# A fused cross-attention and mixture-of-experts layer: low parts of the up weights made ahead, one shared batch moved behind the experts, tables moved

## The chip, the cores and the metric

The kernel runs on one core of a Trainium2 chip. The metric is the device time of one execution in microseconds (us). The core has TensorE (PE, matmuls; PEld is its weight load), VectorE (DVE), ScalarE (ACT), GpSimd (POOL) and SyncE (SP, which here only issues DMAs). Each runs its own instructions in order and waits for the others by semaphores. DMAs are issued from SP's, ACT's and POOL's queues.

## The reference, cut to what matters

```python
x = x + cross_attention(layernorm(x), ctx, ctx)     # x: 4 x 512 x 256, 16 heads, causal: the first 512 context rows count
xf = layernorm(x).reshape(2048, 256)
top, idx = top_k(xf @ gate_w.T, 2)                  # 8 experts, 2 for each row
comb = zeros(2048, 8).at[rows, idx].add(softmax(top))
for e in range(8):                                  # w_up: 8 x 768 x 256 (gate and up), w_down: 8 x 256 x 384
    y = silu(xf @ wg[e].T) * (xf @ wu[e].T) @ w_down[e].T
    out = out + comb[:, e:e + 1] * y
shared = silu(xf @ sg_gate.T) * (xf @ sg_up.T) @ sg_down.T
return x + (shared + out).reshape(4, 512, 256)
```

All inputs and outputs are fp32. There are four batches of 512 rows.

## The kernel before

**Attention** (to about 265 us) takes the heads in NG = 4 groups of four, batch after batch. A loop (`Fori`) runs batches 0 to 2, the last batch is written out by itself. On each engine a function `batch` (PE L767, ACT L1093, DVE L1331, SP L407) holds its part. PE's work of a group is a `slot` (L710): row-maximum scores of the next group (L624, L626) that DVE reduces (L1306) and splits in `max_parts` (L1308), transposed scores of this group (L644) that ACT exponentiates (L1074, `exps`), probabilities times values of the group before (L654) and, near the end of the slot, the maxima's matmuls (L634). The score banks of PE are a ring of three: block j waits until ACT has freed block j - 3. In slots g = 1 and g = 3 of the loop there are also projections (L675) and ACT's and POOL's splitting of their results (`part1`, `part2`, `part3`, ACT L995), whose pieces SP copies into place (`stack`, L390). SP loads one third of the down weights at the end of each loop batch (L432). In the last batch ACT copies the down weights in six pieces to fp32r (`down_hi`, L1059, called out of `exps` after blocks 3 and 7), and DVE subtracts to get the low parts (`down_lo`, L1326).

**Parts.** An fp32 matmul is two instructions in the profile. The experts' matmuls are instead made of fp32r parts: a high part (a copy to fp32r) and a low part (the rest); three matmuls, high x high, high x low and low x high, stand for one.

**The front of the experts** (about 265 to 327 us). `ln2_transposes` and `logits` give the router's input; DVE makes ranks, tiles and slots in a long chain (L1399 to L1504), `in_tile` (L1472), `at_tile` (L1476, L1477) and 32 columns `at_slot` (`hot_slots`, L1480, L1483); PE turns them into lists by 32 matmuls (L898), DVE reduces them to `token_of` (L1504). POOL then gathers rows by indirect DMA (L580). The normalised rows are stored to DRAM first (`xn_d`: SP L445 for batches 0 to 2, ACT L1134 for batch 3), and with them 16 bytes a row of router results (`who`, SP L452). SP loads the up weights (6 MB, `wup`, L450) as soon as attention has let go of their place; ACT copies them to high parts (`hi_parts`, eight pieces), DVE subtracts low parts (`lo_part`, L1486). Meanwhile PE computes the shared expert of batches 0, 1 and 2: `shared_up` (L844; gate and up, three blocks m of four fp32 matmuls on 512 columns, L851), ACT's silu (L1146), DVE's product (`shared_h`, L1405), `shared_down` (L855, 12 fp32 matmuls on 256 columns, L861), DVE's addition (`shared_y`, L1410).

**The expert slots** (327 to 476 us). 39 tiles of 128 gathered rows; in slot t PE transposes the rows of tile t + 1 (L910), transposes hidden of t - 2 (L933), does `down` of t - 3 (nine matmuls of 256 columns, L942 to L944) and `up` of t (12 matmuls of 384 columns, L923 to L925). ACT makes the high parts and the silu, DVE the low parts, the product and the weighted result; POOL adds the results into one of two sums in DRAM (L588).

**The end** (from 476 us). PE does the shared expert of batch 3, SP loads the two sums (L458), DVE adds them (`add_sum`, L1593), adds the shared result (L1606), and ACT stores the output (L1211).

The order that PE's front has, in full (its waits and calls from L890 to L955):

```python
shared_up(0, 2); pe.wait_ge(rank_read, 2); shared_down(0); shared_up(1)
pe.wait_ge(hot_built, 1)          # then the 32 matmuls of the lists
shared_down(1); shared_up(2, 0, 2)
pe.wait_ge(hot_read, 1)
rows_t(0, 0, 0, 1, True); shared_up(2, 2, 3); rows_t(1, 1, 1, 1); shared_down(2)
pe.wait_ge(up_lo, SPLITS)         # then up(0, 0, first[0])
```

Of the kernel before, what the change touches and what calls it, by code (L numbers as in the profile page):

```python
# [28 lines left out]
P = 128  # L29
F32 = mybir.dt.float32  # L30
# [14 lines left out]
def build(nc, x, ctxT, wqT, bq, wkT, bk, wvT, bv, woT, bo, gwT, wupT, wdnT, sgT, suT, sdT, out):  # L45
# [34 lines left out]
    with ExitStack() as ctx:  # L80
# [9 lines left out]
        xn_d = nc.dram_tensor("normed_rows", (N + P, D + WHO), F32, kind="Internal").ap()  # L90
        acc = [nc.dram_tensor(f"sum_rows{i}", (N + P, D), F32, kind="Internal").ap() for i in range(2)]
# [10 lines left out]
        wdn_lo = sb("w_down_lo", [P, M, E * D], F32R)  # L102
        wsg = sb("w_sg", [P, C, HALF])
# [28 lines left out]
        with nc.sbuf_tensor("e_hT_hi", [P, 2, M, P], F32R) as e_hT_hi, \  # L132
                nc.sbuf_tensor("e_hT_lo", [P, 2, M, P], F32R) as e_hT_lo:
            pass
        moe = sb("moe", [P, MOE])
        e_xT_hi = sb("e_xT_hi", [P, 2, C, P], F32R)
# [5 lines left out]
        with nc.sbuf_tensor("ahead_of_router", [P, 24 * KB], F32) as ahead:  # L142
            with nc.sbuf_tensor("router", [P, 24 * KB], F32) as router:
                pass
        ROUTER = 24 * KB
        wup_hi = sb("wup_hi", [P, C, E * 2 * HALF], F32R)
        with nc.sbuf_tensor("wup", [P, C, E * 2 * HALF], F32) as wup:
            pass
        wup_lo = sb("wup_lo", [P, C, E * 2 * HALF], F32R)
        wdn_hi = sb("w_down_hi", [P, M, E * D], F32R)  # L150
# [86 lines left out]
        in_tile = part(NJ * NT // 2).bitcast(BF16).rearrange("p (j t) -> p j t", j=NJ)  # L237
# [3 lines left out]
        tcmp = hot[:, NT * E:2 * NT * E].rearrange("p (t e) -> p t e", e=E)  # L241
        at_tile = part(NJ * NCOL * NT // 2).bitcast(BF16).rearrange("p (j c t) -> p j c t", j=NJ, c=NCOL)
# [3 lines left out]
        ld_k, ld_q, ld_ctx, ld_v, ld_o, ld_cv, ld_moe, ld_up = (sem(n) for n in  # L246
            ("ld_k", "ld_q", "ld_ctx", "ld_v", "ld_o", "ld_cv", "ld_moe", "ld_up"))
        consts, pads, fills, pad_rows = sem("consts"), sem("pads"), sem("fills"), sem("pad_rows")
        xn_stored, acc_zeroed = sem("xn_stored"), sem("acc_zeroed")
# [31 lines left out]
        up_hi, up_lo, wts_ready, e_xhi = (sem(n) for n in ("up_hi", "up_lo", "wts_ready", "e_xhi"))  # L281
# [65 lines left out]
        EARLY = 4  # L347
# [1297 lines left out]
```

## Time and profile before

| | |
|---|---|
| median of 3 runs | 501.17 us (499.0 to 502.9) |
| the profiled execution | 502.17 us, its span 500.3 us |
| TensorE busy | 458.4 us, 92% of the span |
| VectorE, ScalarE, GpSimd busy | 308.2, 210.1, 193.1 us |
| mean granted TensorE clock | 0.982 of full speed |

The profile shows one execution; its times are microseconds from the start of the span. A line number such as L851 is a line of the kernel before. "Busy" counts the time in which an engine has an instruction at work; matmuls are pipelined, so the starts of two neighbours tell more of a matmul's cost than its own duration. The granted clock is a share of TensorE's full speed, 2.4 GHz. In a timeline row the bracket at the end is the idle time before the instruction and what ended it.

### The profile page before, as it was taken

The page shows a single profiled execution, that of the slowest core. Times are in us where ns is not written, and L with a number is a line of the kernel's source. Part 1 is how long each engine was busy: PE and PEld are TensorE (multiplying, and loading weights), DVE is VectorE, ACT ScalarE, POOL GpSimd, SP SyncE. Part 2 cuts the span into 40 slices and gives each one's busy share as a digit, 9 for nine tenths or more (in the row PEclk, how much of TensorE's full clock was granted, in tenths as well). Part 3 has the DMA queues.
Part 4 walks back from the last instruction along what each step waited for, and adds up shares of the span by engine and source line. Part 5 has one row for each costly group of instructions (what it writes and reads, how often), then busy time and mean ns, then how long its engine had stood idle before and what let it go on. Part 6 is the DMA issues. An engine that isn't in the chain of part 4 may idle for free.

```text
span 500.3 us, 10299 instructions
## 1 busy us (share of the span) xinstructions
PE 458.4 (92%) x3154; PEld 318.9 (64%) x3155; DVE 308.2 (62%) x651; ACT 210.1 (42%) x420; POOL 193.1 (39%) x204
## 2 busy tenths in 40 slices
PE   7868999999999999988699799999999999999993
PEld 6644344654447443554256366599999999999852
DVE  4984757477563757656674796855554554555436
ACT  2254666517572566517862352523322322322210
POOL 4123545114541336201512002126666766665420
PEclk9998999999999999999979899999999999999998
DMA  8593322422124121400298900014344344444279
GB/s 263 102 229 107 108 72 65 149 65 73 64 78 145 33 95 47 138 28 2 77 371 292 367 2 21 21 33 65 64 74 74 63 71 70 70 65 74 33 197 338
DMA packets 45574, 53.84 MB, mean 108 GB/s; under 512 B 7760, under 2 KB 41872, under 8 KB 44912
## 3 DMA queue, kind: packets, MB, share of 16 engines
q1 hardware_dynamic: 34320, 39.77, 24.8%
q0 software_dynamic: 7488, 10.31, 12.8%
q10 hardware_dynamic: 3744, 3.47, 2.7%
q8 instruction: 13, 0.21, 0.2%
q14 instruction: 9, 0.07, 0.1%
HBM read 27.09 MB, written 13.67 MB: 81 GB/s over the span
## 4 chain that ended last, share of the span: by engine, by line
PE 68%; DVE 10%; ACT 9%; DMA 6%; issue 5%; SPq 1%; DVEq 0%; ACTq 0%; POOLq 0%
PE set_a L624 7%; PE set_b L654 7%; PE set_a L924 6%; PE set_a L925 5%; PE set_a L923 5%; ACT attention L1074 5%; PE set_a L851 5%; PE set_a L675 4%; PE set_b L644 4%; DVE attention L1306 3%; PE set_b L861 3%; PE set_b L942 3%; PE set_a L832 3%; PE set_b L943 3%; PE set_b L944 3%
## 5 line engine op out<-in xcount | busy, mean ns | idle before, releaser
L1306 DVE TENSOR_REDUCE attention<-set_a 128x2 f32<-128x1024 f32 (+2 forms) x96 | 95.9, 1042 | 28.0 <-PE set_a L626 26.1
L1074 ACT ACTIVATE attention<-set_b 128x512 f32<-128x512 f32 (+1 forms) x176 | 88.4, 570 | 58.5 <-PE set_b L644 45.8
L528 POOL TENSOR_SCALAR_AFFINE_SELECT attention<-attention 128x512 f32<-128x512 f32 x64 | 40.8, 650 | 110.4 <-ACT attention L1074 110.4
L588 POOL DMA_INDIRECT sum_rows<-moe,token_of x39 | 61.8, 1585 | 43.9 <-issue 28.9
L644 PE MATMUL set_b<-attention 99*128 99x512 bf16 (+3 forms) x256 | 60.4, 310 | 13.6 <-ACT attention L1074 10.2
L624 PE MATMUL set_a<-attention 96*128 96x512 bf16 (+3 forms) x256 | 61.5, 306 | 5.6 <-DVE attention L1306 5.4
L580 POOL DMA_INDIRECT e_x<-normed_rows,token_of x39 | 39.4, 1010 | 63.7 <-DVE token_of L1504 37.3
L1173 ACT ACTIVATE moe<-set_a 128x384 f32<-128x384 f32 x39 | 19.1, 490 | 104.9 <-PE set_a L925 104.9
L1529 DVE TENSOR_TENSOR moe<-set_a,moe 128x384 f32<-128x384 f32 x39 | 21.8, 558 | 62.7 <-ACT moe L1173 62.7
L624 PEld LDWEIGHTS set_a<-attention 96*128 96x128 bf16 x256 | 25.3, 99 | 45.3 <-DVE attention L1306 18.0
L923 PE MATMUL set_a<-wup_hi,e_xT_hi 128*128 x156 | 53.1, 340 | 0.0
L924 PE MATMUL set_a<-wup_lo,e_xT_hi 128*128 x156 | 52.9, 339 | 0.0
L925 PE MATMUL set_a<-wup_hi,e_xT_lo 128*128 x156 | 52.8, 338 | 0.0
L626 PE MATMUL set_a<-maskb,identb 128*128 128x128 bf16 x256 | 49.6, 222 | 0.0
L654 PE MATMUL set_b<-attention 128*32 128x128 f32 (+3 forms) x512 | 46.2, 463 | 0.4 <-ACT attention L995 0.3
L644 PEld LDWEIGHTS set_b<-attention 99*128 99x128 bf16 x256 | 19.6, 99 | 37.2 <-ACT attention L1074 24.8
L942 PE MATMUL set_b<-w_down_hi,e_hT_hi 128*128 x117 | 36.4, 311 | 1.3 <-DVE moe L1541 0.8
L995 ACT ACTIVATE attention<-set_b 12x512 bf16<-12x512 f32 (+4 forms) x48 | 25.7, 596 | 22.6 <-PE set_b L820 10.2
L509 POOL TENSOR_TENSOR attention<-attention 128x512 f32<-128x512 f32 x14 | 15.9, 1154 | 47.5 <-ACT attention L995 27.8
L944 PE MATMUL set_b<-w_down_hi,e_hT_lo 128*128 x117 | 32.9, 281 | 0.0
L943 PE MATMUL set_b<-w_down_lo,e_hT_hi 128*128 x117 | 32.9, 281 | 0.0
L995 ACT ACTIVATE attention<-attention 128x512 bf16<-128x512 f32 x32 | 19.4, 644 | 30.9 <-DVE attention L1254 26.2
(167 smaller groups left out, 843.5 us busy)
## 6 DMA issues: line engine op xcount, KB each, us to landing
attention<-attention SPq DMA_DIRECT2D x182, 64.0 KB, 2.6
wup<-in_wupT SPq DMA_DIRECT2D x2, 3072.0 KB, 14.6
sum_rows<-attention SPq DMA_DIRECT2D x2, 2048.0 KB, 13.6
wup<-sum_rows SPq DMA_DIRECT2D x8, 512.0 KB, 7.0
attention<-in_ctxT SPq DMA_DIRECT2D x7, 512.0 KB, 6.2
w_down<-in_wdnT SPq DMA_DIRECT2D x3, 1024.0 KB, 5.0
x_res<-in_x SPq DMA_DIRECT2D x4, 512.0 KB, 7.1
out<-x_res ACTq DMA_DIRECT2D x8, 256.0 KB, 4.0
```

The lines of the kernel that those rows point to most:

```text
L588: g.indirect_dma_start(acc[i], bass.IndirectOffsetOnAxis(token_of[:, t:t + 1], 0), e_y[:, t % 2, :], None, compute_op=ALU.add).then_inc(ad ...
L624: mm(dst, qstack[0:ROWS, g // 2, h, k * P:w], kstack[0:ROWS, g // 2, h, 0:w], start=True, stop=False)
L626: last = mm(dst[:, k * P:w], identb[:], maskb[:], start=False, stop=True)
L644: last = mm(bank(par)[:, i * w:(i + 1) * w], kstack[0:ROWS + 3, g // 2, h, k * P:(k + 1) * P], qstack[0:ROWS + 3, g // 2, h, k * P:S], sta ...
L654: last = mm(pv_bank[32 * h:32 * h + 32, k * P:S], vaug[:, k, HG * g + h, :], pT[k][:, h, :], start=k == 0, stop=k == QT - 1, tile_position ...
L923: mm(dst, e_xT_hi[:, a, c, :], wup_hi[:, c, cols], start=c == 0, stop=False)
L924: mm(dst, e_xT_hi[:, a, c, :], wup_lo[:, c, cols], start=False, stop=False)
L925: last = mm(dst, e_xT_lo[:, a, c, :], wup_hi[:, c, cols], start=False, stop=c == C - 1)
L942: mm(dst, e_hT_hi[:, a, m, :], wdn_hi[:, m, cols], start=m == 0, stop=False)
L943: mm(dst, e_hT_hi[:, a, m, :], wdn_lo[:, m, cols], start=False, stop=False)
L1074: nc.scalar.activation(pT[k][:, h:h + heads, :], bank(par)[:, 0:heads * (S - k * P)], ACT.Exp).then_inc(b_free, 1)
L1306: v.tensor_reduce(dst, src, AX.X, ALU.max, negate=True).then_inc(a_free, 1)
```

## The change

**Up weights' low parts.** In each of the loop's three batches SP loads a third of the up weights (2 MB) into a place of attention's that was free (`ahead`, which shares its memory with `wdn_hi`). In slots g = 2 and g = 3 ACT copies two pieces each to fp32r (`ahead_part`, 128 x 1024, after blocks 2 and 6 of `exps`), and DVE subtracts two pieces each behind `max_parts` (`ahead_low`). SP then stores the low parts (2 MB) to a tensor in DRAM (`up_lo_d`). At the front SP loads them (2 x 3 MB) behind the two loads of `wup`; `lo_part` is gone from DVE, and ACT makes the high parts in one go between the silus of batches 0 and 1.

**Third shared batch.** Batch 2's shared expert moves behind the expert slots, ahead of batch 3's. Gate and up of these two are made of fp32r parts (`shared_up_parts`: 36 matmuls of 512 columns a batch, where 12 fp32 ones were). Their high parts (rows and weights) are four copies on ACT in slots 4 to 7, their low parts four subtractions on DVE in slots 5 to 8; these slots are taken out of the loops.

**Tables.** `at_slot`, `tio`, `tcmp`, `in_tile` and `at_tile` move from memory of their own onto the normalised rows, `at_tile` onto those of batch 3. POOL's `tio` waits for the stores of batches 0 to 2, and DVE waits for that of batch 3 (`xn_last`) ahead of `at_tile`. The `who` store moves from SP's queue to ACT's, behind that of batch 3.

```diff
...
+        sg_end = wup[:, 0, T * D:T * D + M * S].rearrange("p (m n) -> p m n", m=M)
+        x_lo = moe_r[:, T * D:T * D + C * N].rearrange("p (c n) -> p c n", c=C)
+        x_hi = [at.rearrange("p (c n) -> p c n", c=C) for at in
+                (moe_r[:, T * D - C * S:T * D], moe_r[:, T * D + N:T * D + N + C * S])]
+        w_hi = moe_r[:, T * D + C * N:T * D + C * N + 2 * C * HALF].rearrange("p (a c n) -> p a c n", a=2, c=C)
...
+        parts_of(moe, (B - 1) * QT * D)
         hot = part(NJ * P // 2)
         at_slot = hot.bitcast(BF16).rearrange("p (j i) -> p j i", j=NJ)
         tio = hot[:, 0:NT * E].rearrange("p (t e) -> p t e", e=E)
         tcmp = hot[:, NT * E:2 * NT * E].rearrange("p (t e) -> p t e", e=E)
+        in_tile = part(NJ * NT // 2).bitcast(BF16).rearrange("p (j t) -> p j t", j=NJ)
+        size[0] = T * D
         at_tile = part(NJ * NCOL * NT // 2).bitcast(BF16).rearrange("p (j c t) -> p j c t", j=NJ, c=NCOL)
...
+        def ahead_piece(w, k):
+            c, half = divmod(k, AHEAD // C)
+            return w[:, c, half * W_AHEAD // 2:(half + 1) * W_AHEAD // 2]
+
+        def ahead_high(k):
+            return wdn_hi[:, C, k % 2 * W_AHEAD // 2:(k % 2 + 1) * W_AHEAD // 2]
...
+                    sp.dma_start(ahead[:, 0:C, :], wupT.rearrange("(c p) n -> p c n", p=P)[:, :, bass.ds(b * W_AHEAD, W_AHEAD)]
+                                 ).then_inc(ahead_in, DMA)
...
+                    sp.wait_ge(ahead_lo, AHEAD * (b + 1))
+                    sp.dma_start(up_lo_d[:, :, bass.ds(b * W_AHEAD, W_AHEAD)], wdn_hi[:, 0:C, :].bitcast(F32)
+                                 ).then_inc(ahead_out, DMA)
                     sp.wait_ge(b_full, n_b + 3 * B_SLOT)
                     stack(3, 2 * b + 3)
+                    sp.wait_ge(ahead_out, DMA * (b + 1))
                     sp.dma_start(wdn[:, bass.ds(b, 1), :], wdnT[bass.ds(b * P, P)].rearrange("p (o n) -> p o n", o=1)
...
-                sp.dma_start(wup[:, c, :], wupT[c * P:(c + 1) * P]).then_inc(ld_up, DMA)
-            sp.wait_ge(who_ready, TOP_K)
-            sp.dma_start(xn_d[0:N, D:D + WHO].rearrange("(t p) i -> p t i", p=P), who).then_inc(who_stored, DMA)
+                sp.dma_start(wup[:, c, :], wupT[c * P:(c + 1) * P]).then_inc(ld_up[c], DMA)
+            for c in range(C):
+                sp.dma_start(wup_lo[:, c, :].bitcast(F32), up_lo_d[:, c, :]).then_inc(ld_lo, DMA)
...
+            pool.wait_ge(xn_stored, DMA * (B - 1))
+            pool.wait_ge(b_full, B_LN2[2] + C)
+            count(tio, [[1, NT], [0, E]], 0, 0)
 
 
             pool.wait_ge(pad_rows, DMA)
             pool.wait_ge(acc_zeroed, 2 * DMA)
-            pool.wait_ge(xn_stored, DMA * B)
+            pool.wait_ge(xn_last, DMA)
...
+            def shared_up_parts(b):
                 for m in range(M):
+                    n = b * M + m
+                    pe.wait_ge(s_h, n - 1)
+                    for i, (w_lo, dst) in enumerate(zip((wsg_lo, wsu_lo), gu[n % 2])):
+                        for c in range(C):
+                            high, low = w_hi[:, i, c, m * P:(m + 1) * P], w_lo[:, c, m * P:(m + 1) * P]
+                            rows_hi, rows_lo = x_hi[b - 2][:, c, :], x_lo[:, c, b * S:(b + 1) * S]
+                            mm(dst, high, rows_hi, start=c == 0, stop=False)
+                            mm(dst, high, rows_lo, start=False, stop=False)
+                            last = mm(dst, low, rows_hi, start=False, stop=c == C - 1)
+                    last.then_inc(s_up, 1)
...
-            shared_up(1)
+            shared_up(1, 0, 2)
...
             last.then_inc(hot_full, 1)
-            shared_down(1)
-            shared_up(2, 0, 2)
+            shared_up(1, 2)
...
+            shared_down(1, 0, 1)
             rows_t(0, 0, 0, 1, True)
-            shared_up(2, 2, 3)
+            shared_down(1, 1, 2)
             rows_t(1, 1, 1, 1)
-            shared_down(2)
+            shared_down(1, 2)
             pe.wait_ge(experts_known, 1)
             first = [expert(t) for t in range(3)]
-            pe.wait_ge(up_lo, SPLITS)
-            pe.wait_ge(s_h, (B - 1) * M)
+            pe.wait_ge(up_hi, SPLITS)
+            pe.wait_ge(ld_lo, DMA * C)
+            pe.wait_ge(s_h, (B - 2) * M)
             up(0, 0, first[0])
...
-            shared_up(3)
+            pe.wait_ge(end_lo, AHEAD)
+            shared_up_parts(2)
             pe.wait_ge(e_yr, NT + 1)
+            shared_down(2)
+            shared_up_parts(3)
             shared_down(3)
...
+            def ahead_part(b, k):
+                if k == 0:
+                    act.wait_ge(ahead_in, DMA * (b + 1))
+                if k > 1:
+                    act.wait_ge(ahead_lo, AHEAD * b + k - 1)
+                copy(ahead_high(k), ahead_piece(ahead, k)).then_inc(ahead_hi, 1)
...
+                                  b, {2: 2 * g - 4, 6: 2 * g - 3} if g > 1 and not final else {})
...
+                                xn2[:, (B - 1) * QT:T, :]).then_inc(xn_last, DMA)
...
+            shared_silu(0, 0)
+            shared_silu(0, 1)
+            act.wait_ge(who_ready, TOP_K)
+            nc.scalar.dma_start(xn_d[0:N, D:D + WHO].rearrange("(t p) i -> p t i", p=P), who).then_inc(who_stored, DMA)
+            shared_silu(0, 2)
+            act.wait_ge(ld_up[0], DMA)
+            hi_parts(range(0, SPLITS // 2))
+            act.wait_ge(ld_up[1], DMA)
+            hi_parts(range(SPLITS // 2, SPLITS - 2))
+            shared_silu(1, 0)
+            hi_parts(range(SPLITS - 2, SPLITS - 1))
+            shared_silu(1, 1)
+            hi_parts(range(SPLITS - 1, SPLITS))
+            shared_silu(1, 2)
...
+            high_of = ((x_hi[0], xn2T[:, :, 2 * S:3 * S]), (x_hi[1], xn2T[:, :, 3 * S:4 * S]),
+                       (w_hi[:, 0], wsg[:]), (w_hi[:, 1], wsu[:]))
+            for t in range(3, PEEL):
+                slot(t, t % 2)
+                if t - 4 in range(AHEAD):
+                    copy(*high_of[t - 4]).then_inc(end_hi, 1)
...
+            def ahead_low(b, k):
+                dve.wait_ge(ahead_hi, AHEAD * b + k + 1)
+                v.tensor_tensor(ahead_piece(wdn_hi, k), ahead_piece(ahead, k), ahead_high(k),
+                                ALU.subtract).then_inc(ahead_lo, 1)
...
+                    if g in (2, 3) and not final:
+                        for k in (2 * g - 4, 2 * g - 3):
+                            ahead_low(b, k)
...
             shared_h(0, 2)
+            dve.wait_ge(xn_last, DMA)
             v.tensor_tensor(at_tile[:, :, 0, :], in_tile, per_row(row_of), ALU.mult)
             v.tensor_tensor(at_tile[:, :, 1, :], in_tile, per_row(own_lo), ALU.mult)
...
-            shared_y(1)
-
-            lo_part(2)
-            shared_h(2, 0)
-            lo_part(3)
-            lo_part(EARLY)
-            shared_h(2, 1)
+            shared_h(1, 2)
...
+            def end_low(i):
+                dve.wait_ge(end_hi, i + 1)
+                dst, src, high = ((x_lo[:, :, 2 * S:3 * S], xn2T[:, :, 2 * S:3 * S], x_hi[0]),
+                                  (x_lo[:, :, 3 * S:4 * S], xn2T[:, :, 3 * S:4 * S], x_hi[1]),
+                                  (wsg_lo[:], wsg[:], w_hi[:, 0]), (wsu_lo[:], wsu[:], w_hi[:, 1]))[i]
+                v.tensor_tensor(dst, src, high, ALU.subtract).then_inc(end_lo, 1)
...
+                shared_h(2, m)
+            for b in range(B - 2):
+                add_sum(1, slice(b * QT, (b + 1) * QT), (y_in[1][b], DMA))
+            shared_y(2)
+            shared_h(3, 0)
+            dve.wait_ge(s_yfree, B)
+            add_sum(1, slice(2 * QT, 3 * QT), (y_in[1][2], DMA))
+            shared_h(3, 1)
             add_sum(1, slice(T - QT, T), (y_in[1][B - 1], DMA))
+            shared_h(3, 2)
             for c in range(2 * B):
...
```

## Rows read from the trace of the kernel before

**Rows 1.** The page: busy us of each engine, share, instructions.

```profile
PE 458.4 (92%) x3154; PEld 318.9 (64%) x3155; DVE 308.2 (62%) x651; ACT 210.1 (42%) x420; POOL 193.1 (39%) x204
```

**Rows 2.** Windows: length, busy us of each engine, granted clock, DMA share, GB/s.

```profile
284.00:286.00 2.00, 2.00 (x4) 0.86 (x3) 1.81 (x6) 0.00 (x0) 0.00 (x0) 0.53 0.68 226
...
360.00:380.00 20.00, 20.00 (x140) 19.68 (x139) 10.19 (x30) 5.94 (x16) 13.36 (x11) 1.00 0.45 74
```

**Rows 3.** Chain that ended last, in time: start, us, engine, tile, line.

```profile
283.03 5.40 PE set_a L851 x8
...
293.61 10.30 PE set_a L851 x24
...
321.88 5.18 PE set_b L861 x24
...
327.06 0.18 PE set_a L923
...
335.16 0.12 PE set_b L943
```

**Rows 4.** Timeline of ACT in attention: start, us, engine, line, shapes, idle before.

```profile
115.34 1.19 ACT L995 ACTIVATE attention<-attention 128x512 bf16<-128x512 f32 x2
...
123.17 2.62 ACT L1074 ACTIVATE attention<-set_b 128x512 f32<-128x512 f32 x6 [0.64 <-PE set_b L644]
...
238.53 1.06 ACT L995 ACTIVATE w_down_hi<-w_down 128x1024 fp32r<-128x1024 f32 x1
```

**Rows 5.** Timeline of the end, PE and DVE.

```profile
476.01 1.88 PE L851 MATMUL set_a<-moe,w_sg 128*128 128x512 f32 x4
...
491.65 1.29 DVE L1593 TENSOR_TENSOR x_res<-x_res,wup 128x512 f32<-128x512 f32 x2 [0.21 <-DMA wup<-sum_rows]
...
495.84 1.28 DVE L1606 TENSOR_TENSOR x_res<-set_b,x_res 128x512 f32<-128x512 f32 x2
```

**Rows 6.** Timeline of DVE in attention.

```profile
130.75 1.41 DVE L1254 TENSOR_SCALAR attention<-set_a,attention 128x512 f32<-128x512 f32 x2 [5.04 <-PE set_a L675]
...
240.01 5.06 DVE L1328 TENSOR_TENSOR w_down_lo<-w_down,w_down_hi 128x1024 fp32r<-128x1024 f32 x4
```

**Rows 7.** Timeline of PE: maxima matmuls around two slots g = 2.

```profile
115.79 0.39 PE L634 MATMUL set_b<-identb,attention 128*12 128x128 bf16 x4
...
126.07 0.39 PE L634 MATMUL set_b<-identb,attention 128*12 128x128 bf16 x4
...
230.27 0.39 PE L634 MATMUL set_b<-identb,attention 128*12 128x128 bf16 x4
...
241.40 0.39 PE L634 MATMUL set_b<-identb,attention 128*12 128x128 bf16 x4
```

**Rows 8.** Timeline of the front, ACT's queue, DVE and POOL.

```profile
272.77 0.41 ACTq L1134 DMA_DIRECT2D normed_rows<-moe  x1
...
290.70 1.45 DVE L1476 TENSOR_TENSOR router<-router 128x1248 bf16<-128x1248 bf16 x1
...
299.06 1.39 DVE L1483 TENSOR_SCALAR router<-router 128x128 bf16<-128x128 bf16 x8
...
307.12 0.24 DVE L1504 TENSOR_SCALAR token_of<-router 128x39 int32<-128x39 f32 x1
...
308.30 1.15 POOL L580 DMA_INDIRECT e_x<-normed_rows,token_of  x1 [37.27 <-DVE token_of L1504]
```

**Rows 9.** Tile wup: issue (ns, first and last start) and landing (us).

```profile
L450 SPq DMA_DIRECT2D wup<-in_wupT x2: 345/390/434, 268.4 to 268.8; - x2
...
DMA to landing us min/median/max: 10.3/14.6/18.8
```

**Rows 10.** DMA queues, 281 to 284 (packets, MB, share); issue, 268 to 273.

```profile
q1 hardware_dynamic: 48, 1.18, 107.6%
q10 hardware_dynamic: 48, 0.05, 5.4%
...
normed_rows<-moe ACTq DMA_DIRECT2D x1, 512.0 KB, 16.6
```

More of the change, by code:

```diff
@@ L134, in build @@
             pass
+        with nc.sbuf_tensor("moe_parts", [P, MOE], F32R) as moe_r:
+            pass
         moe = sb("moe", [P, MOE])
+        ROUTER = 2068
+        with nc.sbuf_tensor("router", [P, ROUTER], F32) as router:
+            pass
         e_xT_hi = sb("e_xT_hi", [P, 2, C, P], F32R)
@@ L139, in build @@
         e_w = sb("e_w", [P, 2, TOP_K])
[L142 to L146, printed above, removed]
         with nc.sbuf_tensor("wup", [P, C, E * 2 * HALF], F32) as wup:
             pass
+        wup_hi = sb("wup_hi", [P, C, E * 2 * HALF], F32R)
         wup_lo = sb("wup_lo", [P, C, E * 2 * HALF], F32R)
+        with nc.sbuf_tensor("up_ahead", [P, M, E * D], F32) as ahead:
+            pass
         wdn_hi = sb("w_down_hi", [P, M, E * D], F32R)
@@ L1201, in _ @@
             hidden_t(NT - 1, (NT - 1) % 2)
-            for m in range(M):
-                shared_silu(3, m)
+            for b in range(B - 2, B):
+                for m in range(M):
+                    shared_silu(b, m)
             o_t = out.rearrange("b (k p) d -> p (b k) d", p=P)
@@ L1546, in freed @@
                 return added[i], DMA * SUMS[i][t - 1]
[L1548 removed]
             rows_lo(0, 0)
[L1550 to L1551 removed]
             rows_lo(1, 1)
[L1553 removed]
             weights(0, 0, True)
             weights(1, 1, True)
[L1556 removed]
+            shared_y(1)
             hidden(0, 0)
@@ L1571, in slot @@
                 hidden(t, a)
-            for t in range(3, 5):
-                slot(t, t % 2, (t + 1) % NX, None)
-            LOOPS = (NT - 7) // NX
+            def end_low(i):
[4 more added lines that the diff above has]
+                v.tensor_tensor(dst, src, high, ALU.subtract).then_inc(end_lo, 1)
+            PEEL = 9
+            for t in range(3, PEEL):
+                slot(t, t % 2, (t + 1) % NX, freed(t - 3) if t > 4 else None)
+                if t - 5 in range(AHEAD):
+                    end_low(t - 5)
+            LOOPS = (NT - 1 - PEEL) // NX
             with dve.Fori(0, LOOPS) as i:
                 for j in range(NX):
-                    slot(NX * i + 5 + j, (5 + j) % 2, (6 + j) % NX, (added[j % 2], DMA * (2 * i + j // 2 + 1)))
-            for t in range(5 + NX * LOOPS, NT - 1):
+                    slot(NX * i + PEEL + j, (PEEL + j) % 2, (PEEL + 1 + j) % NX,
+                         (added[j % 2], DMA * (2 * i + 2 + j // 2 + 1)))
+            for t in range(PEEL + NX * LOOPS, NT - 1):
                 slot(t, t % 2, (t + 1) % NX, freed(t - 3))
```

83 lines of the change are left out of this document (35 added, 48 removed).

## Prediction, made before the change was run

> **What bounds the kernel now.** I read four views in this order. The page's engine line says that TensorE is busy for 92% of the span [rows 1]. The windows by stage say where that is hard: in the expert slots PE is busy for 20.00 of 20 us, with VectorE at 10.2 and ScalarE at 5.9 [rows 2]. The chain of waits then shows the stretch between attention and experts: from 283.03 to the first expert matmul at 327.06 it is almost all shared-expert matmuls [rows 3], so there too PE is the limit, and the router's lists are ready before PE has time for them. In attention PE is close to full, but its banks are freed by ScalarE's exponentials, which run six in a row with nothing between them [rows 4]; a copy put among them is paid by PE. At the tail the last thing is VectorE's two additions at 495.84, some four microseconds after PE has finished (476.01 + 10.3 + 5.2 = 491.5), because the sums' loads and additions are longer than PE's work there [rows 3, 5]. So four stretches count: attention, the front (283 to 327), the expert slots, the end. The trace's run took 502.17 us for a span of 500.3 and the median of the runs is 501.17; I sum against 502.17 and take off 1.0 for the median.
>
> **Attention: low parts made ahead.** In each of the three loop batches, slots g = 2 and g = 3 get two ScalarE copies and two VectorE subtractions of 128x1024. Both have exact twins in the last batch: one down_hi copy takes 1.06 us [rows 4], and four down_lo subtractions take 5.06 us, some 1.23 each [rows 6]. What a pair of such copies does to a slot can be read from the same slot (g = 2) with and without them, from one set of maxima to the next: 126.07 - 115.79 = 10.28 us in the loop, 241.40 - 230.27 = 11.13 us in the last batch [rows 7]. That is 0.85 us for the pair, but an underestimate: the loop's slot before it already holds part2's two copies (1.19 us [rows 4]) just before its maxima, where the last batch has its second copy, so that copy is partly cancelled. The ceiling is that nothing hides: 2 x 1.06 = 2.12 a slot. Over six slots this is 5.1 to 12.7 us. I take 1.5 a slot, 9.0 us, in the middle: the first copy sits in the run of six, and the second delays the exponential on which the maxima and the last two score blocks wait; in g = 3 it comes on top of part2. It could be nothing only if ScalarE had idle time inside the run, and it has none. The subtractions I cost at nothing: VectorE idles 5.04 us between the end of the maxima's parts and its next operation in g = 2 [rows 6], against 2 x 1.23; if that cover fails, 3 x 2 x 1.23 = 7 us. SP gets a 2 MB load, a wait for the fourth subtraction, a 2 MB store and a wait for it, per batch. Behind the first wait stand the stack DMAs of group 3, which are not needed before slot g = 2 of the next batch, two slots and the batch's own projections later; behind the second the w_down load and the next context load, which are needed later still. Nothing.
>
> **The front: what leaves it.** Batch 2's gate and up (10.30 us for 24 instructions) and down (5.18) leave PE ahead of the experts, 15.5 us [rows 3]; eight subtractions leave VectorE. If the rest kept up, PE would finish gate and up of batch 1's first two blocks at 300.5, build the lists at once, get its first gathered rows at 306 to 307 and start the experts near 312, that is 15 us sooner.
>
> **The front: what ends last in its place.** The tables for the lists move onto the rows of batch 3, so VectorE now waits for their store (xn_last) ahead of the operation that ran at 290.70 [rows 8]. That store is issued on ScalarE's queue at 272.77 [rows 8], while SP's queue is loading the 6 MB of wup, issued at 268.4 and 268.8 [rows 9]. The store took 16.6 us to land [rows 10], at 289.4; the second half of wup took 18.8 [rows 9], to 287.6. So the 0.5 MB landed only when the 6 MB were through. The packet counts say why: in the 3 us from 281, SP's queue moved 48 packets (1.18 MB, 24 KB each) and ScalarE's 48 (0.05 MB, 1 KB each) [rows 10]. They alternate one for one, 16 a microsecond each, and the store has 512 packets. Now 6 MB of low parts follow wup in SP's queue in the same 24 KB rows: 256 packets more, 16 us at that rate, to about 303.5. At 16 a microsecond from 274 on the store alone needs until 306. So it lands with the end of the low parts, near 304.5, and VectorE stands there for 14 us. Behind the wait are the two at_tile products, the 32 hot columns, shared_y(0) and shared_h(1, 0); PE waits for hot_built from 300.5 on, ScalarE for PE, and GpSimd for the lists.
>
> From the operation at 290.70 to the last hot column at 300.45 VectorE worked without a gap, 9.75 us [rows 8]: hot_built comes at 304.5 + 9.75 = 314.3. PE has stood for 14 us by then. After a much shorter stand, just ahead of 283.03, the granted clock was 0.53 from 284 to 286 [rows 2], the lower of the two levels (1.2 GHz), and eight instructions took 5.40 where 3.43 (a third of 10.30) is usual [rows 3]: 2 us lost. So: lists 2.4 after hot_built, gathers 0.95 after token_of is done (308.30 against 307.12 + 0.24 [rows 8]), first rows about 3 us later, at 320.5; PE meanwhile runs batch 1's third gate and up at the lower clock, 316.1 to 321.5, then down and the two transposes, 5.8 us: first expert matmul at 327.3. Before it was 327.06. I put the front at 0, between -3 (no clock loss, store 1 us sooner) and +4. The who store moves behind xn_last on the same queue and is through by 308, ahead of the lists.
>
> **A rule against that.** The rows show one 1 KB packet to one 24 KB packet [rows 10]. The Trainium skill, page "DMA: Bandwidth & Descriptors", section "Queues, rings and completion order", says that a DMA engine takes turns between queues a packet at a time, and that such a packet holds typically some 9 to 17 descriptors. By that rule the store's 32 rows per engine would need 2 to 4 turns of the other queue, land by about 279 and hold nobody up. It landed at 289.4, which speaks against it here; what it would give is the first rival.
>
> **The expert slots.** Four copies and four subtractions go into peeled slots. A slot is some 3.8 us (476.01 less 327.06, over 39) with ScalarE at 30% and VectorE at 51% [rows 2], so each (about 1.06 and 1.23) fits beside PE. I take 0.3 in all; the ceiling is 4 us. The loops' other parts are the same.
>
> **The end.** Batch 2 joins batch 3 behind the experts. A matmul of 384 columns in fp32r takes 0.18 us and one of 256 columns 0.12 [rows 3], so I estimate 0.24 for 512; 36 of them are 8.6 us a batch, in place of 10.30 (7.7 if 0.18 and 0.12 hold a fixed part that doesn't grow). PE then has 8.6 + 5.2 + 8.6 = 22.4 us to the end of the last gate and up, and silu and product take 1.4 more. Behind that product VectorE has eight additions of 0.65 (1.29 for two [rows 5]), 5.2, as long as the last down on PE: the final additions start 29.0 us after the last expert matmul. Before, they started at 495.84 - 476.01 = 19.8 us after it [rows 5]. That is +9.2; with 0.3 off, since the last output store no longer shares the queue with seven others, +8.9 (7.3 to 10). Before, PE's extra work would have been covered for 4 us by the sums' loads; I have counted that cover as used up.
>
> **Sum.** 9.0 + 0 + 0.3 + 8.9 = 18.2: 502.17 + 18.2 = 520.4, less 1.0 for the median: 519.
>
> **Rivals.** (A) The store isn't late: its rows go several to a turn while the low parts load, VectorE goes on at 290.7, the front gains 15 and the sum is 519 - 15 = 504, no change that can be told. What decides is whether xn_last lands before 291. For it: by 289.4 it had landed in the run before, so little has to improve; against it, the 48 to 48 and the 16.6 us. (B) The store is late, but the attention copies are hidden, at 1.5 us in all: 511.5, still slower; against it, the 0.85 a slot of the last batch. (C) One cover for both: ScalarE's copies fall into time that PE owes to others and the store lands early: 504 - 8 = 496, faster. It needs A and B together. (D) The front is worse, with PE at the lower clock into the first slots: 523.
>
> **Chances.** The forecast (with D) 0.60, A 0.17, B 0.10, C 0.13. About 1% (5 us) is what a measurement of this kernel can tell from no change. So slower by over 1% is forecast, D and B, 0.70; within 1% A, 0.17; faster C, 0.13. The range takes in all but C and the low edge of A: 503 to 525; the likeliest case alone has 513 to 525.
>
> **What would show it.** VectorE idle for some 14 us, ended by the store to the normalised rows, ahead of the product at at_tile; PE idle from gate and up of batch 1 to the lists' matmuls, then a granted clock near 0.5; first expert matmul (relative to the end of attention) where it was; slots g = 2 and 3 of the loop 1 to 2 us longer each; 29 us between the last expert matmul and the final additions. A first expert matmul 10 us or more earlier would make the forecast wrong, and so would slots g = 2 of 10.28 us as before.

## The result, and the profile after

The changed kernel takes 524.59 us (median of 4 runs, 523.13 to 525.69), beside 501.22 us for the kernel before on the same chip. The ratio is 1.0467, with a 95% interval of 1.0419 to 1.0516: slower by 4.7%, where 519 was forecast. Its profiled execution took 524.41 us for a span of 522.5, so the span grew by 22.2.

Four marks cut both spans into the stages that the prediction used: the start of attention's last addition into `x_res`, the first and the last expert matmul, and the end of the span. The stages were read in this way in every kernel that follows:

| kernel | median us | attention, to its last addition | front, to the first expert matmul | expert slots | end | span |
|---|---|---|---|---|---|---|
| before | 501.2 | 267.1 | 59.6 | 149.2 | 24.4 | 500.3 |
| after | 524.6 | 281.1 | 58.2 | 150.8 | 32.4 | 522.5 |
| difference | | +14.0 | -1.4 | +1.6 | +8.0 | +22.2 |
| predicted | | +9.0 | 0 | +0.3 | +8.9 | +18.2 |

The engine line of the page, and the window of 24 us in the expert slots (columns as in [rows 2]):

```profile
PE 458.9 (88%) x3178; PEld 324.8 (62%) x3179; DVE 314.7 (60%) x659; ACT 224.4 (43%) x436; POOL 195.9 (37%) x204
```

```profile
356.00:380.00 24.00, 23.20 (x155) 21.83 (x154) 16.81 (x42) 9.97 (x24) 15.48 (x12) 1.00 0.41 67
```

PE has as many busy microseconds as in [rows 1] (458.4), in a longer span: what was added is waiting, not work. In the expert slots that prepare the end's parts it is busy for 23.20 of 24 us, where it had no gap before [rows 2].

**Attention.** Maxima matmuls mark the slots, as in [rows 7]. First the timeline of PE in the changed kernel, around a slot g = 2, a slot g = 3 and the slot behind it:

```profile
123.00 0.39 PE L666 MATMUL set_b<-identb,attention 128*12 128x128 bf16 x4
...
132.46 0.72 PE L676 MATMUL set_b<-attention 99*128 99x384 bf16 x2 [1.09 <-ACT attention L1134]
...
134.22 0.39 PE L666 MATMUL set_b<-identb,attention 128*12 128x128 bf16 x4
...
148.88 0.39 PE L666 MATMUL set_b<-identb,attention 128*12 128x128 bf16 x4
...
151.10 0.40 PE L676 MATMUL set_b<-attention 99*128 99x128 bf16 x4 [1.13 <-ACT attention L1134]
...
160.10 0.39 PE L666 MATMUL set_b<-identb,attention 128*12 128x128 bf16 x4
```

Attention's last addition, on DVE's timeline (267.12 before):

```profile
281.09 1.23 DVE L1449 TENSOR_TENSOR x_res<-set_a,x_res 128x1024 f32<-128x1024 f32 x1 [4.64 <-PE set_a L864]
```

Then what ScalarE does in the slot g = 2:

```profile
130.37 0.60 ACT L1134 ACTIVATE attention<-set_b 128x512 f32<-128x512 f32 x1 [0.64 <-PE set_b L676]
130.87 1.05 ACT L1047 ACTIVATE w_down_hi<-up_ahead 128x1024 fp32r<-128x1024 f32 x1
131.81 1.73 ACT L1134 ACTIVATE attention<-set_b 128x512 f32<-128x512 f32 x4
133.40 1.09 ACT L1047 ACTIVATE w_down_hi<-up_ahead 128x1024 fp32r<-128x1024 f32 x1
```

The same marks, and the same block, in the kernel before ([rows 7] has the mark at 126.07):

```profile
124.31 0.72 PE L644 MATMUL set_b<-attention 99*128 99x384 bf16 x2 [0.15 <-ACT attention L1074]
...
139.35 0.39 PE L634 MATMUL set_b<-identb,attention 128*12 128x128 bf16 x4
...
149.63 0.39 PE L634 MATMUL set_b<-identb,attention 128*12 128x128 bf16 x4
```

The slot from 123.00 takes 11.22 us (10.28 before). The two copies stand among the exponentials, and PE's score block at 132.46 waits 1.09 us for one of these; in the kernel before, the same block waits 0.15. The difference, 0.94, is the whole growth of the slot. The slot g = 3 takes 14.66 instead of 13.28, and the one behind it, which begins with the second copy's delay (1.13 against 0.57 at its first blocks, after 0.32 more), 11.22 instead of 10.28. Together 3.26 a loop batch, 9.8 in three. That leaves 4.2 of the 14.0. Batch 0 has the rest: its slot g = 2 takes 16.61 us, 5.4 more than the same slot of batch 1. PE's timeline there, with the first matmul after a gap, and then the windows before and after that:

```profile
56.61 0.39 PE L666 MATMUL set_b<-identb,attention 128*12 128x128 bf16 x4
...
64.72 0.60 PE L676 MATMUL set_b<-attention 99*128 99x512 bf16 x1 [2.89 <-DMA attention<-attention]
...
73.22 0.59 PE L666 MATMUL set_b<-identb,attention 128*12 128x128 bf16 x4
```

```profile
56.60:65.00 8.40, 4.94 (x40) 1.88 (x40) 3.41 (x3) 3.21 (x7) 3.98 (x5) 0.97 0.97 208
65.00:75.00 10.00, 9.80 (x57) 5.25 (x56) 6.32 (x9) 7.22 (x13) 2.02 (x2) 0.51 0.19 57
```

PE waits 2.89 us for a DMA in attention, and then runs ten microseconds at 0.51, the lower of its two levels. The matmul after the gap is the first transposed score of the slot, which by the kernel's code waits for the row of the slot's maxima (`max_in`): a DMA of 12 KB that ScalarE issued at 58.75.

```profile
58.75 0.77 ACTq L1090 DMA_DIRECT2D attention<-attention  x1
```

Up to that gap the DMA engines are full (0.97). The issues of 47 to 60 us (KB each, median us to landing) say with what: SP's 2 MB load, issued at 49.50, has gone ahead of SP's stack DMAs, which landed in 2.8 us in this stretch of the kernel before and land in 5.8 now.

```profile
up_ahead<-in_wupT SPq DMA_DIRECT2D x1, 2048.0 KB, 10.0
attention<-attention SPq DMA_DIRECT2D x14, 64.0 KB, 5.8
```

The two queues' packets (number, MB, share) in the 6 us from the issue of the small DMA show it among these:

```profile
q1 hardware_dynamic: 1140, 0.95, 98.2%
q10 hardware_dynamic: 15, 0.01, 1.3%
```

Its 15 packets go in two parts, ten before 62 and five after 63; in the kernel before, the 15 of the same DMA went within 0.3 us. Why the second part came so much later no run shows.

(The first slots of batch 0 happened to be 1.5 shorter than before and the last batch 0.2 longer: 9.8 + 5.4 - 1.5 + 0.2 = 14.0, to a tenth.)

**The front.** The timeline of the stretch that [rows 3, 8] show for the kernel before, and then the issues of the two stores:

```profile
286.62 0.41 ACTq L1197 DMA_DIRECT2D normed_rows<-moe  x1
...
317.68 1.46 DVE L1558 TENSOR_TENSOR moe<-moe,router 128x1248 bf16<-128x1248 bf16 x1 [13.05 <-DMA normed_rows<-moe]
...
327.50 2.26 PE L946 MATMUL set_b<-moe 128*128 128x78 bf16 x32 [13.32 <-DVE moe L1565]
...
339.33 0.43 PE L970 MATMUL set_a<-wup_hi,e_xT_hi 128*128 x1
```

```profile
normed_rows<-moe ACTq DMA_DIRECT2D x1, 512.0 KB, 31.0
normed_rows<-router ACTq DMA_DIRECT2D x1, 32.0 KB, 23.7
```

The store of batch 3's rows, issued at 286.62, lands 31.0 us later; VectorE stands 13.05 us for it, and PE 13.32 us for VectorE's hot columns. The queues' packets (number, MB, share) in the three microseconds from 294 and from 309 show why: SP's queue, with rows of 24 KB, and ScalarE's, with rows of 1 KB, move 48 and 48. In the single microsecond from 294 they move 16 and 16, one row of each on each of the 16 engines.

```profile
q1 hardware_dynamic: 48, 1.18, 92.5%
q10 hardware_dynamic: 48, 0.05, 5.3%
...
q1 hardware_dynamic: 48, 1.18, 91.4%
q10 hardware_dynamic: 48, 0.05, 4.6%
```

From 315 on, when the loads are through, what is left in ScalarE's queue moves alone: 1744 packets in 3 us but 0.05 MB, the last rows of the store and the 16-byte rows of the `who` store behind it. The store lands at 317.6. So 13 us of standing replaces the 15 us of shared-expert work that left [rows 3], and the first expert matmul comes 58.2 us after attention instead of 59.6.

**The end.** PE's timeline behind the last expert matmul, and VectorE's last additions (before: [rows 5]):

```profile
490.21 0.39 PE L895 MATMUL set_a<-moe_parts 128*128 128x512 f32 x1
490.44 0.40 PE L896 MATMUL set_a<-moe_parts 128*128 128x512 f32 x1
490.67 0.40 PE L897 MATMUL set_a<-moe_parts,w_sg_lo 128*128 128x512 f32 x1
...
518.43 1.28 DVE L1689 TENSOR_TENSOR x_res<-set_b,x_res 128x512 f32<-128x512 f32 x2
```

One fp32r product of 512 columns follows the other in 0.23 us; the last additions start 28.2 us after the first of them, where it was 19.8.

### The profile page after: what moved, and what is told of

It reads as the page before. It is cut to its first block, busy times and chain, and to the rows that moved or that the text cites. A ratio compares the mean times of both kernels' runs of the same rounds, so it can differ in the third digit from the quotient of the medians.

```text
span 522.5 us, 10358 instructions
## 1 busy us (share of the span) xinstructions
PE 458.9 (88%) x3178; PEld 324.8 (62%) x3179; DVE 314.7 (60%) x659; ACT 224.4 (43%) x436; POOL 195.9 (37%) x204
## 4 chain that ended last, share of the span: by engine, by line
PE 62%; DVE 11%; ACT 10%; DMA 9%; issue 6%; SPq 1%; ACTq 0%; DVEq 0%
PE set_a L656 6%; DMA normed_rows<-moe 6%; ACT attention L1134 5%; PE set_a L971 5%; PE set_a L970 5%; PE set_a L972 5%; PE set_b L686 5%; PE set_a L707 4%; PE set_b L676 3%; PE set_b L989 3%; DVE attention L1378 3%; PE set_a L864 3%; PE set_b L990 3%; PE set_b L991 3%; PE set_b L980 2%
## 5 line engine op out<-in xcount | busy, mean ns | idle before, releaser
L1134 ACT ACTIVATE attention<-set_b 128x512 f32<-128x512 f32 (+1 forms) x176 | 89.5, 568 | 59.5 <-PE set_b L676 46.0
L559 POOL TENSOR_SCALAR_AFFINE_SELECT attention<-attention 128x512 f32<-128x512 f32 x64 | 44.4, 706 | 119.5 <-ACT attention L1134 119.5
L676 PE MATMUL set_b<-attention 99*128 99x512 bf16 (+3 forms) x256 | 61.7, 317 | 24.4 <-ACT attention L1134 18.3
## 6 DMA issues: line engine op xcount, KB each, us to landing
wup<-sum_rows SPq DMA_DIRECT2D x8, 512.0 KB, 6.9
attention<-in_ctxT SPq DMA_DIRECT2D x7, 512.0 KB, 8.8
```

Source lines behind the costliest of these rows:

```text
L676: last = mm(bank(par)[:, i * w:(i + 1) * w], kstack[0:ROWS + 3, g // 2, h, k * P:(k + 1) * P], qstack[0:ROWS + 3, g // 2, h, k * P:S], sta ...
L1134: nc.scalar.activation(pT[k][:, h:h + heads, :], bank(par)[:, 0:heads * (S - k * P)], ACT.Exp).then_inc(b_free, 1)
```

## The experiments

Theory after the result: three separate costs, each with its own place, make the kernel slower: the load of low parts at the front (13 us, behind which the rows' store alternates), the copies in the slots (9.8), and SP's first 2 MB load (5.4). The end costs 8, which the front's 15 would more than pay. The rivals were that the front is bound by something else behind the store, that a slot's growth comes from the subtractions or the DMAs, and that the end's new form gains nothing. The ratios are to the kernel before, measured beside the experiments: 501.98 us for the first four, 502.31 for the other three. Each stage is read from one profiled execution.

**The loads of low parts wait for the rows' store.**

```diff
             for c in range(C):
                 sp.dma_start(wup[:, c, :], wupT[c * P:(c + 1) * P]).then_inc(ld_up[c], DMA)
+            sp.wait_ge(xn_last, DMA)
             for c in range(C):
```

> The kernel after, with one wait added on SP: the loads of the low parts are issued only when batch 3's store (xn_last) has landed. My theory: that store lands late (31 us after its issue) because it shares the DMA engines with 12 MB of 24 KB rows one packet for one packet; without the second 6 MB it lands as in the kernel before, some 17 us after its issue, VectorE's 13 us wait ahead of at_tile is gone, and the experts start some 13 us sooner. The low parts then land some 16 us after the store, before PE wants them. Time: 524.6 - 13 = 511 to 512. Rival (the lists are late for another reason, such as the who store behind it or the gathers): less than 3 us gained.

512.04 us, ratio to the kernel before 1.019 (1.014 to 1.0239). The store landed 15.8 us after its issue instead of 31.0, and the front shrank from 58.2 to 44.3. So the store was what bound the front, and with it early nothing else held the experts back within these 14 us. Up to 300 us `wup` itself was still loading, and there the queues alternated as before, 49 to 48 packets in 3 us; in the 4 us from 300, with `wup` nearly through, ScalarE's queue moved 0.42 MB (2455 packets, most of them the 16-byte rows of `who`).

**The same loads in rows of 3 KB.**

```diff
-                sp.dma_start(wup[:, c, :], wupT[c * P:(c + 1) * P]).then_inc(ld_up[c], DMA)
+                for j in range(8):
+                    at = slice(j * CUT, (j + 1) * CUT)
+                    sp.dma_start(wup[:, c, at], wupT[c * P:(c + 1) * P, at]).then_inc(ld_up[c], DMA)
...
```

(The loads of `wup_lo` are cut in the same way; CUT is 768 columns.)

> The kernel after, with the loads of wup and of its low parts each cut into 8 DMAs of 768 columns (rows of 3 KB in place of 24 KB), same queue, same bytes, same order, no wait added. If the queues share packet for packet (my theory), the store of 512 rows of 1 KB needs 32 turns an engine at some 4 KB a turn, near 24 GB/s an engine: 5 to 6 us, so it lands 6 to 9 us after its issue with 12 MB still being loaded; VectorE does not wait, time 511 to 512. Rival (the queues share by bytes, or the store is held until what was issued before it is through): it still lands 17 to 31 us after its issue, and the time stays within 3 us of 524.6 or goes to 512 only through a shorter load.

511.83 us, ratio 1.019 (1.0152 to 1.0228), the front 43.7 us: as good as waiting, though nothing waits. The rows' store landed in 10.5 us, somewhat later than expected, but VectorE did not wait for it. The queues' packets in the 3 us from 294, with SP's rows now 3 KB long:

```profile
q1 hardware_dynamic: 327, 0.89, 74.0%
q10 hardware_dynamic: 322, 0.33, 30.9%
```

Again one row to one row, but ScalarE's queue now moves 0.33 MB in the time in which it moved 0.05. Here it is the length of the other queue's rows that sets how long the store of short rows takes beside it.

**Batch 0's load ahead of attention.**

```diff
+            def load_ahead(b):
+                sp.dma_start(ahead[:, 0:C, :], ...)
+
+            load_ahead(0)
...
-                    sp.dma_start(ahead[:, 0:C, :], ...)
...
-            with sp.Fori(0, B - 1) as b:
+            with sp.Fori(0, B - 2) as b:
                 batch(b, False)
+                load_ahead(b + 1)
+            batch(B - 2, False)
```

> The kernel after, with batch 0's load of up weights (2 MB) issued at the start of the program, behind the load of the values' bias, in place of at the start of batch 0; the other two stay where they were. In the trace after, slot g = 2 of batch 0 is 16.6 us from maxima to maxima where batches 1 and 2 have 11.2, with PE waiting 2.9 us on the row of maxima's DMA and a granted clock of 0.5 behind it. My theory: the 2 MB hold up the stack copies, and these hold up that small DMA on the other queue; with the load gone from there this slot is 11.2 too. Time: 524.6 - 5.4 = 519. Rival (the slot is long because ScalarE waits for the load itself, or the first pass of a loop is slow anyway): no change, or slower.

521.59 us, ratio 1.0365 (1.0321 to 1.0409). That is 3.0 us less than the changed kernel, where 5.4 was expected. Batch 0's slot g = 2 took 11.23 us, as in the other batches, and PE did not wait for the small DMA. With the load in its old place it waited 2.3 to 3.3 us in four traces of six (the changed kernel's and those of the low loads that wait, the 3 KB rows and no copies); the other two are taken up at the run without subtractions. So the load is what held that slot up. But attention ended only 1.9 us earlier: the slot behind g = 3 took 12.80 and 12.82 us instead of 11.22 in two batches. The window of one of them, below the same slot of the changed kernel:

```profile
148.88:160.10 11.22, 9.40 (x85) 4.35 (x84) 8.26 (x12) 7.96 (x17) 5.42 (x7) 1.00 0.55 219
```

```profile
145.35:158.17 12.82, 11.00 (x85) 4.72 (x84) 8.27 (x12) 7.96 (x17) 5.43 (x7) 0.87 0.58 215
```

PE is busy for 1.6 us more with as many matmuls at a clock of 0.87: the lower level, for a few microseconds. It follows the two waits for ScalarE at the slot's start (0.32 and 1.13 us); the same two waits, as long, are in the changed kernel, where the clock stayed at 1.00. In the six traces that keep the copies in the slots, 9 of the 18 slots behind a g = 3 in the loop took 12.8 us, one or two in each trace but the changed kernel's own; in the three without (before, no copies, all three places), none of nine did. So in an execution the copies there cost 9.8 us and, in these traces, none to two times 1.6 us of clock on top.

**No copies in the slots.**

```diff
-                                  b, {2: 2 * g - 4, 6: 2 * g - 3} if g > 1 and not final else {})
+                                  b, {})
...
-                dve.wait_ge(ahead_hi, AHEAD * b + k + 1)
-                v.tensor_tensor(ahead_piece(wdn_hi, k), ahead_piece(ahead, k), ahead_high(k),
+                if k == 0:
+                    dve.wait_ge(ahead_in, DMA * (b + 1))
+                v.tensor_tensor(ahead_piece(wdn_hi, k), ahead_piece(ahead, k), ahead_piece(ahead, k),
```

> The kernel after without ScalarE's 12 copies to high parts in attention; VectorE subtracts the loaded weights from themselves, so the low parts are zero (this part of the computation is left out); loads, stores and subtractions stay. My theory: the 3.27 us by which each loop batch has grown (0.94, 1.38, 0.94 us in slots 2, 3 and 4) are the copies standing among the exponentials; without them loop batches take 57.7 us again and the time is 524.6 - 9.8 = 515. Rival (VectorE's subtractions or the DMAs lengthen the slots): slots stay 0.9 to 1.4 us longer than before, less than 3 us gained.

514.12 us, ratio 1.0221 (1.0169 to 1.0274). The slots went back to 10.28, 13.28 and 10.28 us, a loop batch to 57.7, with the loads, stores and subtractions still there. PE's block that had waited 1.09:

```profile
128.07 0.72 PE L676 MATMUL set_b<-attention 99*128 99x384 bf16 x2 [0.15 <-ACT attention L1134]
```

So ScalarE's copies were the 9.8. Batch 0's slot g = 2 still took 15.0 us, 2.50 of it PE's wait for the maxima's DMA: that cost is not the copies'.

**No subtractions.**

```diff
-                    if g in (2, 3) and not final:
-                        for k in (2 * g - 4, 2 * g - 3):
-                            ahead_low(b, k)
...
-                    sp.dma_start(up_lo_d[:, :, bass.ds(b * W_AHEAD, W_AHEAD)], wdn_hi[:, 0:C, :].bitcast(F32)
+                    sp.dma_start(up_lo_d[:, :, bass.ds(b * W_AHEAD, W_AHEAD)], ahead[:, 0:C, :]
...
```

(ScalarE's copies now signal `ahead_lo` themselves and wait for no subtraction.)

> The copies stay on ScalarE and the stores stay on SP, but VectorE makes no subtractions in attention: the raw weights are stored as low parts (so the low-part products of the expert slots are those of other numbers). My theory, that the subtractions lie in VectorE's idle stretches of a slot: attention ends where it does in the changed kernel (281.1 us, loop batch 61.0), time 524 +- 2. The rival, that part of the 3.3 us by which a loop batch grew is the subtractions': a loop batch of 58 to 59.5 us, attention ends 5 to 9 us earlier, time 515 to 519.

525.05 us, ratio 1.0449 (1.0411 to 1.0487): no change against the changed kernel. VectorE's twelve subtractions are hidden. Attention ended at 281.9, but with another split: batch 0's slot g = 2 took 11.22, while its first slot (clock 0.67) and two of those behind g = 3 (0.87 each, 12.80 us) ran in part at the lower clock. The 2 MB load stands where it stood and landed at 58.7 (issued at 49.72, 9.0 us). But after its slower first slots PE came to slot g = 2 at 59.60 instead of 56.61, ScalarE issued the maxima's DMA at 61.74, and PE did not wait for it; in the changed kernel the load landed at 59.5 and that DMA was issued at 58.75, ahead of it. With gate and up at the end in fp32 it was as here. So the load costs PE this wait only in executions in which the two meet. With the copies in place the disturbances move from slot to slot between executions, and the end of attention hardly does (279.2 to 283.2 in all kernels that keep them there).

**Gate and up at the end in fp32.**

```diff
-            pe.wait_ge(end_lo, AHEAD)
-            shared_up_parts(2)
+            shared_up(2)
...
-            shared_up_parts(3)
+            shared_up(3)
...
-                if t - 4 in range(AHEAD):
-                    copy(*high_of[t - 4]).then_inc(end_hi, 1)
...
-                if t - 5 in range(AHEAD):
-                    end_low(t - 5)
```

> Gate and up of the last two shared batches are fp32 again, each behind the experts' last down product; the copies and subtractions for their parts leave the expert slots. My theory: the 72 products in fp32r parts (0.2335 us each, 16.8 in all) become 24 in fp32 at about 0.86 (20.6), so the tail behind the experts grows by about 3.8 us, and the expert slots lose the 1.6 us that they grew by: time 526 to 528. The rival, that the fp32r parts at the end cost as much as they save because their operands or rounding wait: time 520 to 524, with the tail no longer than in the changed kernel.

526.99 us, ratio 1.0486 (1.0436 to 1.0535). PE's timeline there, fp32 with four matmuls a row:

```profile
489.11 1.88 PE L883 MATMUL set_a<-moe,w_sg 128*128 128x512 f32 x4
490.83 1.88 PE L883 MATMUL set_a<-moe,w_su 128*128 128x512 f32 x4
```

A block of four records (two fp32 products) goes by in 1.72 us; the end took 36.2 us instead of 32.4, and the expert slots 148.9 instead of 150.8. The end grew by the 3.8 that was expected, and the slots gave back 1.8 where 1.6 was: the fp32r form at the end gains 2 us net by the stages, and the four copies and subtractions that prepare it are all of what the slots lost. The medians differ by 2.4 us, less than the runs of this kernel among themselves (523.4 to 529.4), so the net gain rests on the stages.

**All three places at once.** The same work as the changed kernel, elsewhere: the low loads wait as in the first experiment; a batch's load of ahead weights comes after its first stacking and its store at the batch's end; copies and subtractions stand between the batches. SP's loop is written out for it.

```diff
+            sp.wait_ge(xn_last, DMA)
...
+                    if b:
+                        sp.wait_ge(ahead_out, DMA * b)
+                    sp.dma_start(ahead[:, 0:C, :], ...)
...
-                                  b, {2: 2 * g - 4, 6: 2 * g - 3} if g > 1 and not final else {})
+                                  b, {})
...
+                    for k in range(2):
+                        ahead_part(b, k)
...
+                    for k in range(2, AHEAD):
+                        ahead_part(b, k)
...
```

> The same work, placed otherwise: the loads of the low parts wait for the last store of normed rows; a batch's load of ahead weights is issued after its first run's stacking, its store waits at the batch's end; the copies and subtractions run between the batches instead of in the slots of g = 2 and 3. If the three costs are as the first four runs put them (13 at the front, 9.8 in the slots, 5.4 in the first batch), all of them go and the time is 524.6 - 28 = 496 to 498, below the kernel before. The rival: the copies (4 x about 0.9 us of ScalarE and as much of VectorE) stand on the path between the batches as well, 1 to 3 us a batch, and the stacks meet the moved load: loop batches of 59 to 61 us, time 503 to 511.

497.30 us (6 runs, 494.96 to 498.38), ratio to the kernel before 0.9897 (0.9867 to 0.9926): 1.0% less than the kernel before, a small gain whose interval lies clear of 1, and 27.3 us below the changed kernel. By the medians the three costs had come to 12.6, 10.5 and 3.0 when taken away one by one, 26.1 together. A loop batch took 57.8 us. ScalarE's timeline between two batches, and the same two waits in the kernel before:

```profile
153.33 2.00 ACT L1048 ACTIVATE w_down_hi<-up_ahead 128x1024 fp32r<-128x1024 f32 x2
156.73 1.15 ACT L1048 ACTIVATE attention<-set_b 128x384 f32<-128x384 f32 x3 [1.39 <-PE set_b L853]
157.75 2.02 ACT L1048 ACTIVATE w_down_hi<-up_ahead 128x1024 fp32r<-128x1024 f32 x2
165.91 1.29 ACT L1048 ACTIVATE attention<-attention 128x512 bf16<-128x512 f32 x2 [6.14 <-DVE attention L1332]
```

```profile
156.51 1.15 ACT L995 ACTIVATE attention<-set_b 128x384 f32<-128x384 f32 x3 [3.29 <-PE set_b L820]
...
165.69 1.29 ACT L995 ACTIVATE attention<-attention 128x512 bf16<-128x512 f32 x2 [8.03 <-DVE attention L1254]
```

Each pair takes 2.0 us, and ScalarE's wait behind it is shorter by 1.9 (1.39 for 3.29, 6.14 for 8.03), so the copies stand in time that nobody needs; in the slots the same four stood in a run in which PE waits for every exponential. The stages of all kernels, as in the first table:

| kernel | median us | attention | front | expert slots | end |
|---|---|---|---|---|---|
| low loads wait | 512.0 | 282.5 | 44.3 | 150.5 | 32.4 |
| 3 KB rows | 511.8 | 283.2 | 43.7 | 150.6 | 32.4 |
| first load early | 521.6 | 279.2 | 58.2 | 150.2 | 32.5 |
| no copies | 514.1 | 271.1 | 59.6 | 150.8 | 32.4 |
| no subtractions | 525.1 | 281.9 | 58.3 | 150.9 | 32.5 |
| end in fp32 | 527.0 | 281.9 | 58.2 | 148.9 | 36.2 |
| all three | 497.3 | 267.4 | 44.9 | 150.5 | 32.4 |

The last line has the front of the first and an attention as short as before the change; its end and slots still carry the +8.0 and +1.4 that the third shared batch costs there, against 14.7 that it saves at the front.

## Why the prediction was right, and where not

The sign and the mechanisms that the forecast rests on held. 524.6 lies inside the range, 0.4 us from its upper edge (525), and the four runs reach from 523.13 to 525.69: that the range held is in part luck. By its steps:

- **The store behind the low parts: right, and it decided the result.** Forecast were one row of 1 KB for one of 24 KB, a landing 37.4 us after attention's last addition (304.5 against 267.12), and 14 us for VectorE. Measured were 48 to 48, 36.5 us and 13.05. Rival A, by which the store lands early, fell: at 24 KB in three kernels and at 3 KB in one the queues moved one row each in turn, 16 and 16 within a microsecond. The Trainium skill (page "DMA: Bandwidth & Descriptors", section "Queues, rings and completion order") has some 9 to 17 descriptors to a turn, and these traces do not agree. The 279 that the prediction worked out by that rule was wrong in itself: it lets the store's rows go several to a turn, but the long rows one to a turn. Were both queues to take many rows a turn, then by an estimate from the rows the long ones, at about 1 us each (48 on 16 engines in 3 us), would keep the store late as well.
- **The front: 0 forecast, -1.4 measured.** The landing was 0.9 earlier than worked out, and from hot_built on it took PE 11.8 us to the first expert matmul where 13.0 was counted. PE's clock after its stand was 0.50, as expected.
- **The copies: right, 9.0 forecast and 9.8 measured in the changed kernel's trace** (to which other traces add 1.6 or 3.2 of clock, which was not forecast). The split was not: 0.94 and 1.38 in slots g = 2 and g = 3 (1.5 each was taken), and 0.94 in the slot after, which was not counted.
- **The subtractions: right.** Nothing, as the run without them shows.
- **"Nothing" for SP's load and store: wrong, by 5.4 us in the profiled execution and 3.0 between the medians.** This is the step that failed. It looked only at what is queued behind SP's two waits. It left out the 2 MB load itself, which fills the DMA engines and stands in SP's queue ahead of the stack DMAs. ScalarE's 12 KB of maxima, in the other queue, came late among these rows: PE's wait for it, 2.89 us, and the lower clock that followed were 5.4 us of batch 0. In batches 1 and 2 the load cost nothing: without the copies the slots had their old lengths.
- **The expert slots: mis-sized.** 0.3 was taken with a ceiling of 4, since each operation was said to fit beside PE; the eight operations cost 1.6 to 1.8. That ScalarE is busy for 30% and VectorE for 51% of a slot did not mean that 1.06 and 1.23 us fit in.
- **The end: right, 8.9 forecast and 8.0 measured.** The product of 512 columns takes 0.2335 us against an estimate of 0.24, the additions start 28.2 us after the last expert matmul against 29.0, and from them to the end it is 4.1 us instead of 4.5, where 0.3 was taken off.

The terms miss by +5.0 (attention), -1.4, +1.3 and -0.9, which is +4.0 of the 5.6 between 519 and 524.6. The rest is the step from a profiled run to the median: 1.0 was taken off, as for the kernel before, but the changed kernel's profiled run lies 0.2 below its median; rounding is the remainder. Rival C (both covers, 496, faster) did not happen in this kernel; the last experiment makes that case by moving the loads and the copies, and it came to 497.3.

What stays open is why the lower clock strikes after some of PE's waits of about 1.4 us in a slot and not after others that are as long; no run here tells them apart. That the waits bring it on is read from what precedes it, and from its absence where the copies are gone. Nor was it tried what each of the last experiment's moves brings alone, beyond the runs above that take away its cost.

## What to carry to other kernels

A transfer that something waits for should not share the DMA engines with a long-rowed load that nobody needs yet: hold that load back behind the urgent store, or cut its rows; the one gave back 12.6 us here, the other 12.8. Free time on an in-order engine is worth something only where it lies: four copies cost 3.3 us a batch in a run in which each operation releases the next engine, and nothing some microseconds later, between the batches. And of a DMA that is added, ask what is behind it in its own queue and on the same engines, not only what is behind the waits that come with it.

## What the runs showed that was not expected

A store of 512 KB takes 10.5, 15.8 or 31.0 us by what loads beside it, in a kernel otherwise the same. Short waits of TensorE cost more than they last: 2.89 us of waiting for a DMA was followed by ten microseconds at a granted clock of 0.51, and the slot lost 5.4 us; waits of 0.32 and 1.13 us were followed by 1.6 us lost to the clock in 9 slots of 18, and by none in the others.
